# Attention kernel: where a key tile's context products stand in the order of TensorE, and how the softmax maxima of a group reach the query stack

## What is computed

```
x = layernorm(x + self_attention(x))        # 16 heads of 16, scores + log_pen, softmax, times V
x = layernorm(x + cross_attention(x, ctx))  # 16 heads of 16, mask, softmax, times V, output projection
x = layernorm(x + ffn(x))                   # 704 hidden, silu gate, both sides fake-quantised to 8 bits
log_pen = log(max(res * scope, 1e-32))      # per pair of positions, from a sigmoid gate of the rows
```

## Time and profile before

| what | value |
|---|---|
| median of 3 runs | 767.98 us (767.71 to 767.99) |
| the profiled execution | 767.94 us |
| its span | 765.8 us |
| busy share: TensorE, VectorE, ScalarE, GpSimd | 86%, 79%, 63%, 43% |

### The profile page before, as it was taken

How to read it: one execution, slowest core, us unless ns; L and a number is a source line. 1 busy time by engine, 2 the same in 40 slices (tenths; PEclk the granted TensorE clock), 3 DMA queues, 4 the chain that set the end, 5 groups by cost and what they waited for, 6 DMA issues and landing times.

```text
span 765.8 us, 10404 instructions
## 1 busy us (share of the span) xinstructions
PE 657.3 (86%) x3348; PEld 264.6 (35%) x3350; DVE 602.5 (79%) x1299; ACT 479.6 (63%) x800; POOL 325.9 (43%) x417
## 2 busy tenths in 40 slices
PE   7478889999899899998899998999888899885862
PEld 3233324443233243343233432443223244232331
DVE  4987988688988986689987865569985887816986
ACT  4425656556658778654568787454577776873864
POOL 6206767466764414645653144556514011001503
PEclk9678999999999999999999999999999999997967
DMA  3832352310423314312205223232214310000003
GB/s 96 202 72 87 101 131 93 84 27 23 104 72 86 88 42 113 86 45 71 72 24 137 56 73 94 50 110 84 74 40 115 95 45 3 7 1 0 1 0 110
DMA packets 35748, 53.83 MB, mean 70 GB/s; under 512 B 5232, under 2 KB 26736, under 8 KB 35696
## 3 DMA queue, kind: packets, MB, share of 16 engines
q1 hardware_dynamic: 35696, 53.18, 26.2%
HBM read 36.91 MB, written 14.68 MB: 67 GB/s over the span
## 4 chain that ended last, share of the span: by engine, by line
PE 44%; DVE 21%; POOL 16%; issue 9%; ACT 7%; DMA 1%; SPq 0%; POOLq 0%; DVEq 0%; ACTq 0%
POOL probs L737 12%; PE ps L1586 10%; PE ps L1539 8%; PE ps L1562 7%; PE ps L1423 5%; PE ps L1526 4%; ACT probs L922 4%; DVE dist L1029 3%; PE ps L1519 3%; DVE mx L1026 2%; DVE stats L1051 2%; PE ps L1567 1%; PE ps L1566 1%; DVE x L1066 1%; POOL parts L768 1%
## 5 line engine op out<-in xcount | busy, mean ns | idle before, releaser
L1539 PE MATMUL ps<-KS,QS 96*128 96x512 bf16 x512 | 200.2, 394 | 33.6 <-DVE mx L1029 12.8
L922 ACT ACTIVATE probs<-ps 128x512 f32<-128x512 f32 x256 | 149.2, 596 | 124.4 <-PE ps L1567 87.6
L737 POOL TENSOR_TENSOR probs<-probs,penT 128x512 f32<-128x512 f32 x128 | 167.6, 1330 | 111.8 <-ACT probs L922 111.8
L1562 PE MATMUL ps<-QS,KS 108*128 108x512 bf16 x512 | 195.7, 384 | 10.2 <-ACT probs L922 5.3
L1026 DVE TENSOR_REDUCE mx<-ps 128x1 f32<-128x512 f32 x256 | 168.5, 682 | 45.6 <-PE ps L1539 45.0
L922 ACT ACTIVATE probs<-ps,mask_col 128x512 f32<-128x512 f32 x256 | 167.1, 689 | 44.9 <-PE ps L1562 42.6
L1029 DVE CUSTOM_DVE_ANT_0 dist<-ps,mask_rest 128x512 bf16<-128x512 f32 x192 | 125.9, 683 | 24.4 <-PE ps L1539 24.1
L1539 PEld LDWEIGHTS ps<-KS,QS 96*128 96x128 bf16 x512 | 50.5, 99 | 178.8 <-DVE mx L1029 62.1
L1562 PEld LDWEIGHTS ps<-QS,KS 108*128 108x128 bf16 x512 | 49.9, 98 | 89.7 <-ACT probs L922 53.3
L1586 PE MATMUL ps<-probs,v_s 128*32 128x512 f32 x512 | 68.2, 604 | 14.6 <-POOL probs L737 14.3
L1586 PE MATMUL ps<-probs,v_c 128*32 128x512 f32 x512 | 69.1, 612 | 0.9 <-ACT probs L922 0.9
(11 more groups left out here) (191 smaller groups left out, 940.9 us busy)
## 6 DMA issues: line engine op xcount, KB each, us to landing
parts_qs<-parts SPq DMA_DIRECT2D x8, 384.0 KB, 2.7
parts_ks<-parts SPq DMA_DIRECT2D x8, 384.0 KB, 3.0
KS<-parts_ks SPq DMA_DIRECT2D x16, 192.0 KB, 3.6
QS<-parts_qs SPq DMA_DIRECT2D x16, 192.0 KB, 4.0
parts_kc<-parts SPq DMA_DIRECT2D x8, 384.0 KB, 3.0
KS<-parts_kc SPq DMA_DIRECT2D x16, 192.0 KB, 3.0
parts_qc<-parts SPq DMA_DIRECT2D x8, 384.0 KB, 3.0
QS<-parts_qc SPq DMA_DIRECT2D x16, 192.0 KB, 3.5
```

The lines of the kernel that those rows point to most:

```text
L737: g.tensor_tensor(probs[:, T % NP, :], probs[:, T % NP, :], penT[:, MUL_KT.index(kt), :], ALU.mult)\
L922: s_.activation(probs[:, T % NP, :], ps[:, exp_bank(T), :], ACT.Exp, bias=bias)\
L1539: mm(ps[:, MAX_BANKS[(TG * n + i) % AHEAD], :], QS[0:SK, slot, j, t * P:(t + 1) * P], KS[0:SK, slot, j, :], start=True, stop=True).then_in ...
L1562: ins = mm(o, KS[0:SM, slot, j, kt * P:(kt + 1) * P], QS[0:SM, slot, j, :], start=True, stop=not logged)
```

## The change

Two edits. The context products of key tiles 0, 1 and 2 stand behind the exponential product of index 7, 11 and 15 in place of 6, 10 and 14, one slot later (slots 15, 3 and 7); key tile 3 stays in slot 10. And the maxima of a group are turned by one transposition with 48 columns (4 query tiles x 3 parts x 4 heads) in place of four with 12; `mT` is 48 x 128 in place of 12 x 512, and four transfers of 12 x 4 x 128, each on its own `dma_start`, take the place of one of 12 x 4 x 512. The waits on the transfer's semaphore count four times as far.

```diff
--- before.py
+++ after.py
@@ -340,7 +340,7 @@
         mrest = sb("mrest", [P, NT, GH], F32, att)
         mparts = sb("mparts", [P, NT, PARTS, GH], BF16, att)
         own_rows = sb("own_rows", [VC, GH], BF16, att)
-        mT = sb("mT", [PARTS * GH, S], BF16, att)
+        mT = sb("mT", [NT * PARTS * GH, P], BF16, att)
         oT = sb("oT", [P, S], F32, att)
         rsum = sb("rsum", [P, NT, GH], F32, att)
         ctxt = {w: sb("ctx_" + w, [P, NT, H], F32, att) for w in "sc"}
@@ -585,8 +585,11 @@
             def load_shift(n):
 
                 used(sp, unit[("m", n)])
-                sp.dma_start(QS[SK:SM, n % RING, :, :], mT[:, :].unsqueeze(1).broadcast_to((PARTS * GH, GH, S)))\
-                    .then_inc(shift_loaded, 16)
+                rows = PARTS * GH
+                for t in range(NT):
+                    sp.dma_start(QS[SK:SM, n % RING, :, t * P:(t + 1) * P],
+                                 mT[t * rows:(t + 1) * rows, :].unsqueeze(1).broadcast_to((rows, GH, P)))\
+                        .then_inc(shift_loaded, 16)
 
             def load_weight(n):
                 src = a[("w_gate", "w_up", "w_down")[n]]
@@ -887,8 +890,8 @@
                     n = job[1]
                     if n:
 
-                        act.wait_ge(shift_loaded, 16 * n)
-                    copy_out(mT[:, :], bank_bf(u)[0:PARTS * GH, 0:S], u)
+                        act.wait_ge(shift_loaded, 16 * NT * n)
+                    copy_out(mT[:, :], bank_bf(u)[0:NT * PARTS * GH, 0:P], u)
                 elif what == "oT":
                     n = job[1]
                     act.wait_ge(pv_done, NT * (n + 1))
@@ -1482,10 +1485,8 @@
                     products(u, i, c2T, W["o"], halves)
                 elif what == "m":
                     pe.wait_ge(shift_made, job[1] + 1)
-                    for t in range(NT):
-                        ins = tr(bank_bf(u)[0:PARTS * GH, t * P:(t + 1) * P],
-                                 mparts[:, t, :, :].rearrange("p a b -> p (a b)"), ident_b[:, :])
-                    ins.then_inc(side_full[u % 2], 1)
+                    tr(bank_bf(u)[0:NT * PARTS * GH, 0:P], mparts[:, :, :, :].rearrange("p t a b -> p (t a b)"),
+                       ident_b[:, :]).then_inc(side_full[u % 2], 1)
                 elif what == "last_context":
                     context(job[1], NT - 1)
                 elif what == "norm":
@@ -1545,7 +1546,7 @@
                 kt, j, slot, T = i // GH, i % GH, n % RING, TG * n + i
                 if i == 0:
 
-                    pe.wait_ge(shift_loaded, 16 * (n + 1))
+                    pe.wait_ge(shift_loaded, 16 * NT * (n + 1))
                     if n < RING:
                         pe.wait_ge(own_rows_made, n + 1)
                 logged = kind == "s" and kt not in MUL_KT
@@ -1602,7 +1603,7 @@
                     e = s.exp_at(i)
                     if e:
                         exp_tile(*e)
-                        if e[1] % GH == 2 and e[1] > GH:
+                        if e[1] % GH == GH - 1 and e[1] > GH:
                             context(e[0], e[1] // GH - 1)
                     for job in s.items[i]:
                         do(job)
```

## The result

The changed kernel takes **775.03 us** (median of 4 runs, 774.06 to 776.68), the kernel before 767.85 us on the same chip (766.59 to 767.99). The ratio is 1.0098, with a 95% interval of 1.0083 to 1.0113: 7.2 us slower by the medians and 7.5 by the ratio. The forecast was 770.8 us in a range of 758 to 779, with slower by over 0.2% the likeliest. The profiled execution's span is 773.4 us.

What follows compares the result with a forecast made beforehand. TensorE, busy 86% of the span, was taken to set the pace. Contexts -8.1, unevenness +1, transposition -2.3 and transfers +12.3 summed to +2.9 us on 767.94: 770.8 us, range 758 to 779.

Steps and rivals of the forecast that it cites:

- The context's move: Context products one slot later shorten TensorE's waits for GpSimd: -8.1 us, with +1 us for uneven spacing.
- nothing they need is late there: Products put ahead of a waiting context run unhindered for 0.87 us; each of 13 self-group waits loses up to that.
- the -8.1: Gain from moved contexts: 10.1 us of TensorE's waits for GpSimd go, of which 0.8 is counted.
- the +1: Cost of contexts no longer standing four slots apart, bounded by 0 to 2 us; the exponential and maximum banks about cover it.
- The transfers: Four issues of 0.82 us on SyncE's queue land the last transfer too late for slot 8's product: +12.3 us.
- The two attentions' places cancel here: Moving contexts leaves the work between job m and slot 8 the same in both orders; no change in time there.
- so the room stays: Time from the maxima copy's end to slot 8's product is unchanged by the move; 4.67 to 6.84 us in 18 groups.
- Absorption: In five late groups TensorE waits for VectorE a few slots later anyway: 4 us off the transfers' new waits.
- rival B: New waits before slot 8 mostly absorbed by later VectorE waits, contexts give all 10.1 us: 764 us, 17% chance.
- One transposition: One maxima transposition takes 0.219 us where four take 0.39; counted in 18 groups: -2.3 us.
- A: Rival: the four transfers' issues on SyncE's queue are cheap, 0.45 us each: 758 us, 20% chance.
- C: Rival: late landing of the transfers paid in full, context move gives half: 780 us, 15% chance.

Runs made afterwards that it cites:

- experiment 4: Contexts of key tiles 0, 1, 2 and also 3 one slot later, four slots apart again, one transfer, four transpositions, against the kernel before: 769.71 us, ratio 1.0023.
- experiments 1 and 3: Against the kernel before: 1 moved only the contexts of key tiles 0, 1 and 2, 767.48 us; 3 moved only those where GpSimd multiplies the probs, 760.67 us.
- the complement: Contexts one slot later only where GpSimd has no part (cross groups, key tile 1 of self groups), against the kernel before: 771.41 us, ratio 1.0048.
- experiment 2: One transposition of 48 columns and four transfers, contexts left where they were, against the kernel before: 776.38 us, ratio 1.0108.
- experiment 5: The kernel compared here: old four transpositions and old copy, transfer cut into four by columns, against the kernel before: 780.94 us, ratio 1.0165.

## Why the prediction was right, and where its terms were off

The sign and the range held, and the dear issues and late landings of the four transfers are there as forecast. The size was not: 7.2 to 7.5 us for 2.9. A range of 21 us is wide beside that, so that the number lies inside it says little for the sum. Two terms were off, in opposite ways, and the clock, which the sum leaves out, added its part.

**The context's move, forecast -7.1 us with the unevenness, measured -0.4.** The step "nothing they need is late there: VectorE and ScalarE are empty during such a wait" held in the places it was read from. In the group of the earlier trace rows the wait of 1.76 us became one of 0.90, and 0.89 was forecast:

```profile
475.62 1.07 PE L1587 MATMUL ps<-probs,v_s 128*32 128x512 f32 x8 [0.90 <-POOL probs L740]
```

And the gain at GpSimd's tiles alone, 7.1 us, is close to the -8.1. The step that failed is the next one: the +1 for what the move costs where there is no wait for GpSimd. I looked for that cost in the spacing, and even spacing (experiment 4) leaves all of ScalarE's new waits; and I wrote that two exponential banks cover it "about". They don't: a context is what gives ScalarE the time for two exps, and one slot later it stands behind the product that needs that time. By experiments 1 and 3 this term is between 4 us (the complement by itself) and 7 (all contexts less GpSimd's), and the complement's 7.3 us of waits, with the clock left out, speak for the upper end. The edit moved 96 contexts. I costed the 32 that GpSimd has a part in; the other 64 (48 of cross groups, 16 of key tile 1 of self groups) had nothing to gain and something to lose.

**The transfers, forecast +12.3 with 0.82 us an issue.** Right in kind: 128 issues of 0.78 us, a wait in 12 places and 12.6 us in experiment 2, where 12 to 17 us in 12 to 15 places were forecast. In the changed kernel itself it is 7.7 us in 7 places, and the step that failed there is "The two attentions' places cancel here" and "so the room stays": the work between job m and slot 8 is the same, but the moved contexts bring new waits into it (1.0 us for ScalarE in two groups), and the room widens. Off in size: the last landed 2.03 us behind its issue's start for 2.4, and the spacing was 0.84 for 0.87, so each late group was 0.5 us less late than I had. Transposition and transfers together came to +8.3 for +10.0.

**Absorption, forecast 4 us off.** In experiment 2 the waits for VectorE fell by 2.1 us only, and those for GpSimd rose by 2.5, which rival B's "against" had named. So the waits give nothing net absorbed: this step failed, and the earlier landing hid it.

**One transposition**: 0.24 us for 0.39 together, as costed; the copy took 0.271 us, where 0.29 was interpolated. What the term of -2.3 was worth by itself no run shows; beside four transfers the transposition and the shorter copy were worth 4.6 us (experiment 5 against 2).

**The clock, no term of the sum.** The changed kernel ran 20.5 us at the lower level where the kernel before ran 6.8. At half speed that is up to 6.8 us of TensorE's work, and its busy time shows 5.4. Two of the three added stretches stand at waits for the transfer, which the forecast counted without any clock behind them. That the waits caused them isn't shown.

**The rivals.** A (cheap issues) falls with the first row of the issues. B named absorption and full gain at the contexts: neither. C was the dearest end of both terms; the contexts gave even less than its half, the transfers cost less than its full. The sum of +2.9 against +7 came short because the transfers' smaller cost (1.7 us less) didn't make up for the contexts' missing gain (6.7 us). The Trainium skill's sentence on initiation being small beside the DMA ("DMA: Bandwidth & Descriptors", Issuing engines are not separate DMA queues) does not hold for small transfers in a row here: 0.78 against 2.03 us from an issue's start to the landing, and the train is most of the 4.54.

## What to carry to other kernels

Move only the instructions whose wait you have read: each of the others may be covering somebody, as the 64 here did, and a block that depends on nothing (here 1 us of context products) belongs ahead of the product that waits for a slower engine, not behind it. Cutting a transfer in four multiplies its issue, not its bytes; count the issues up to the last one against the room before its first reader. And when a gain and a loss are forecast for two edits of one change, run them apart: here a third of the moved contexts was worth 7 us once the rest stayed where they stood. Then look at the granted clock beside the waits: here two kernels whose waits differ by 7.3 us differ by 3.7 in time.

## What was not expected of the hardware

- The issue of this transfer on SyncE's queue depended on its rows: 780 ns for 12 rows with four repeats, 714 for 12 plain rows, 595 for 16 rows with repeats, and not on its bytes (12 x 4 x 512 and 12 x 4 x 128 both have a minimum of 778 ns; 16 rows 586 and 585). More rows were cheaper. Why isn't settled: only 12 and 16 were tried.
- A transfer of 12 KB between two places of SBUF had landed 2.03 us behind its issue's start, one of 48 KB 2.52. No row shows harm done by rows of 256 bytes.
- In the trace of the changed kernel, TensorE's granted clock went to 0.50 in a wait of 2.98 us and stayed there for 6.8 us; in the kernel before, at the same place with a wait of 1.60 us, for 3.4 us.
